# The recurrence's projections as four products of 32 weight columns

## The reference

```python
q  = einsum('mbtd,dk->mbtk', tx, w_q) * scale            # 128 columns, 4 heads of 32
k  = einsum('mbtd,mdk->mbtk', tx, w_k)
v  = einsum('mbtd,mdk->mbtk', tx, w_v)                   # 256 columns, 4 heads of 64
gk = log_sigmoid(einsum('mbtr,mrk->mbtk', einsum('mbtd,mdr->mbtr', tx, w_gk1), w_gk2) + b_gk) / 16
def step(S, inp):                                        # for each memory, batch and head
    qt, kt, vt, gt = inp
    S = S * exp(gt)[..., None] + kt[..., None] * vt[..., None, :]
    return S, einsum('...k,...kv->...v', qt, S)
```

## Time and profile before

| | us |
|---|---|
| median of three timed runs | 2658.96 |
| lowest and highest | 2658.64, 2659.07 |
| the profiled execution | 2684.99 |
| its span | 2683.3 |

### The profile page before, as it was taken

One profiled execution on the slowest core, in us unless ns is written; L12 is line 12 of the kernel. 1 busy time (PEld: TensorE's weight loads), 2 busy tenths in 40 slices (PEclk: granted clock), 3 DMA queues, 4 the chain that ended last, 5 costly groups with the idle time before them and its releaser, 6 DMA issues. The chain is left out here.

```text
span 2683.3 us, 111106 instructions
## 1 busy us (share of the span) xinstructions
PE 2124.7 (79%) x45872; PEld 1600.7 (60%) x45872; DVE 1836.9 (68%) x4507; ACT 1561.9 (58%) x3824; POOL 1531.6 (57%) x3168
## 2 busy tenths in 40 slices
PE   8788888888888888888868944389999998687793
PEld 5456566566566665556637734366766776565682
DVE  6578888887878887884544555276777777575456
ACT  5577777777777777772433322266666665454231
POOL 3357666666766666768554546544444444256452
PEclk9889999999999999999988965699999999789897
DMA  6911111111121111113346654301111111542546
GB/s 216 265 33 40 40 40 40 40 40 40 41 63 39 40 40 40 40 29 120 138 113 209 197 172 153 109 22 47 51 50 51 49 41 35 199 169 89 154 146 225
DMA packets 188851, 245.89 MB, mean 92 GB/s; under 512 B 41672, under 2 KB 144981, under 8 KB 187456
## 3 DMA queue, kind: packets, MB, share of 16 engines
q1 hardware_dynamic: 161824, 182.08, 22.7%
q0 software_dynamic: 19872, 50.41, 5.5%
q10 hardware_dynamic: 6656, 6.31, 0.8%
HBM read 136.08 MB, written 106.50 MB: 90 GB/s over the span
## 5 line engine op out<-in xcount | busy, mean ns | idle before, releaser
L666 ACT ACTIVATE at_E<-at_S,at_mn 128x1024 f32<-128x1024 f32 (+7 forms) x704 | 594.2, 847 | 211.3 <-DVE at_mn L737 178.2
L737 DVE TENSOR_REDUCE at_mn<-at_S 128x1 f32<-128x1024 f32 (+3 forms) x448 | 494.0, 1104 | 152.6 <-PE at_S L846 152.3
L846 PE MATMUL at_S<-am_sk,am_sq 96*32 96x512 bf16 (+3 forms) x4608 | 395.8, 350 | 1.1 <-ACT at_Tt L656 1.0
L887 PE MATMUL at_pcs<-at_E,at_c 128*32 128x256 f32 (+1 forms) x4864 | 375.7, 338 | 0.0
L605 POOL TENSOR_TENSOR at_kvo<-am_kh,am_vh 128x256 f32<-128x256 f32 x512 | 304.2, 628 | 0.0
L887 PEld LDWEIGHTS at_pcs<-at_E,at_c 128*32 128x32 f32 x4864 | 229.7, 109 | 41.2 <-issue 0.2
L1360 POOL DMA_INDIRECT expert_out<-m_ysb,m_dst x158 | 155.5, 984 | 139.3 <-issue 76.7
L887 PE MATMUL at_pcs<-at_Tt,at_c 128*32 128x128 f32 x1024 | 189.8, 274 | 42.3 <-ACT at_pcs_s L679 42.3
L590 POOL TENSOR_TENSOR at_half<-at_half 128x128 f32<-128x128 f32 (+4 forms) x640 | 185.6, 290 | 50.1
L864 PE MATMUL at_M<-am_ident,at_Tt 128*32 128x64 f32 x8192 | 154.5, 225 | 68.9 <-ACT at_kvr L691 43.1
L656 ACT ACTIVATE at_Tt<-at_S,at_mn 128x192 f32<-128x192 f32 x512 | 174.1, 428 | 48.3 <-DVE at_mn L725 48.1
(11 more groups left out here) (393 smaller groups left out, 5579.9 us busy)
## 6 DMA issues: line engine op xcount, KB each, us to landing
m_xg<-expert_rows SPq DMA_DIRECT2D x158, 129.0 KB
am_sq<-q_parts SPq DMA_DIRECT2D x192, 64.0 KB, 2.3
am_sk<-k_parts SPq DMA_DIRECT2D x192, 64.0 KB, 2.3
memory_rows<-m_blank SPq DMA_DIRECT2D x16, 516.0 KB
gl_hx<-memory_rows SPq DMA_DIRECT2D x32, 258.0 KB, 3.6
m_wgu<-in_f_wgu SPq DMA_DIRECT2D x2, 4096.0 KB
rt_yin<-expert_out SPq DMA_DIRECT2D x7, 1024.0 KB, 11.4
fn_yin<-expert_out SPq DMA_DIRECT2D x7, 1024.0 KB, 8.9
```

What stands on the lines that cost most here:

```text
L666: ins = nc.scalar.activation(E[:, at:at + w], S[v % NS_B][:, i * CW:i * CW + w], ACT.Exp, bias=mn[:, q, s, 1 + j:2 + j], scale=-1.0, accum ...
L737: nc.vector.tensor_reduce(mn[:, q, :, :].rearrange("p s k -> p (s k)")[:, at[0]:at[0] + 1], S[v % NS_B][:, 0:w], AX.X, ALU.min).then_inc(s ...
L846: ins = nc.tensor.matmul(S[v % NS_B][x, at:at + cw], sq[:, u, t * P + x.start:t * P + x.stop], sk[:, u, c0 + c:c0 + c + cw], start=True, s ...
L887: ins = nc.tensor.matmul(pcs[j * R:(j + 1) * R, cols[0]:cols[1]].rearrange("p (b c) -> p b c", c=P), lhsT, rhs, start=(n, j) not in touche ...
```

## The change

In the helper `two` each matmul is issued as four, one for every 32 columns of the stationary operand; each writes its own 32 partitions of the same PSUM tile. `STRIP` is 32. The moving operand is the same for all four. The calls of `two`, their order and the semaphores stay as they are; the increment rides on the last strip.

```diff
--- before.py
+++ after.py
@@ -2537,7 +2537,9 @@
 
             def two(out, lhs, rhs):
                 for k in range(KC):
-                    ins = nc.tensor.matmul(out, lhs(k), rhs(k), start=(k == 0), stop=(k == KC - 1))
+                    for t in range(0, P, STRIP):
+                        ins = nc.tensor.matmul(out[t:t + STRIP, :], lhs(k)[:, t:t + STRIP], rhs(k), start=(k == 0),
+                                               stop=(k == KC - 1))
                 return ins
 
             def rows_T(a):
```

## The result

The changed kernel takes 2685.6 us (median of 9 runs, 2672.59 to 2688.94) where the kernel before takes 2659.07 in the same comparison: ratio 1.0093, 95% interval 1.0077 to 1.011, 26.5 us slower. The forecast was 2659.5 with a range to 2672.

What follows compares the result with a forecast made beforehand. The prediction took the VectorE and ScalarE chain to set the pace, TensorE adding only when delayed. Query -2, first chunk's products -0.5, instruction supply +3 gave +0.5 us on 2658.96: 2659.5, range 2649 to 2672.

Steps and rivals of the forecast that it cites:

- the loads would stand alone: Last rival: in the edited products, strips run one after another, each weight load alone; 272 us more, 2930; chance 0.01.
- The clock stayed: Rival on TensorE in the recurrence: tighter groups keep the clock up, three waits of 3 us go; 2650; chance 0.10.
- VectorE's wait for the logarithm: Sign in the profile after: VectorE's idle for ScalarE's logarithm in the recurrence stays near 95 us.
- The gain of TensorE: Edited products in strips free 1.1 us per own chunk, 1.0 per shared one, 25.6 us over the loop, mostly hidden.
- the first rival: TensorE is the bound of the recurrence after all, so all 25.6 us count: 2633; chance 0.10.
- against this stands the supply of instructions: Cost term in the recurrence: 26 more instruction packets make TensorE pause; taken as +3 us, bounds 0 and 22.6.
- 26 x 0.87 = 22.6 us: Upper bound of the instruction supply cost in the recurrence: each of 26 new packets brings one unhidden pause of 0.87 us.
- 4.0 us for a packet: Mean spacing of instruction packets in the recurrence after the change, in place of 4.9; held well over the pauses seen.
- cover for 0.7 of a chunk: TensorE lacks cover in only some 7 of 23 us of a chunk, so 0.3 of the pauses count: 6.8 us.
- The third rival: Instructions come too late between the gate's end and the first half's scores: 11 to 14 us longer, 2672; chance 0.21.
- The test I set: VectorE's wait for scores in the recurrence stays near 30 us; below 15 means a gain, over 45 a loss.
- carried it over unchanged: The profiled execution's 26 us above the median of timed runs was kept: 2685.5 for the profile, 2659.5 for the median.

Runs made afterwards that it cites:

- x9: The kernel before, unedited, timed and profiled again on one of the faster chips: ratio 1.0001, profile 2660.31 us.
- x10: The changed kernel, unedited, timed and profiled again on one of the faster chips: ratio 1.0098 to the kernel before, profile 2685.55 us.
- x8: The changed kernel with the output products (lines 2670 and 2675) whole instead of in four strips, both halves of a chunk: ratio 1.0041 to the kernel before.
- x6: The kernel before with the output products (lines 2670 and 2675) whole instead of in four strips, both halves of a chunk: ratio 1.0066.
- x2: The kernel before with only the gate product in strips, on a chip where the kernel before takes 2677 or 2682 us (S): ratio 1.0024.
- x4: The kernel before with only the key product in strips, on a chip where the kernel before takes 2677 or 2682 us (S): ratio 1.0077.
- x7: The kernel before with 256 fulfilled waits, 128 instructions, added once ahead of the phase's first product: ratio 1.006.
- x5: The kernel before with 24 fulfilled waits behind each of the helper's 544 calls, 6528 more instructions: 3137.23 us, ratio 1.1807.
- x12: The kernel before with strips only in the first chunk's value product, 96 more instructions once, in front of the loop: ratio 1.0025.

## Why the prediction was wrong

**Right.** 49136 matmuls; 26 packets more in the whole program, 135 for 138 in the same 550 us; the strips overlap. By the rule of the Trainium skill, page "TensorE: Matmul & The Clock Gate", section "Part 3: Packing small matmuls — row/col tiling", as the prediction applied it, the loads would stand alone; the gate's 64 matmuls and 64 loads of 0.11 us took 1.86 us, so the rows do not agree with it. The clock stayed, 0.98 over the phase as in the earlier trace rows. VectorE's wait for the logarithm stayed (87.9 and 86.7 us in x9 and x10). The gain of TensorE was sized a little high: by the groups after, gate 0.13, query 0.07, key 0.4, value 0.13, 0.73 us for an own chunk where I had 1.1. Hardly any of it was to count, and x8 bears that out: its loop is no shorter than x6's. (TensorE was busy for 89.7% of the phase by the earlier trace rows, 493.34 of 550 us, and not for over 90% as the first rival says.)

**The step that failed** is "against this stands the supply of instructions", +3 us with an upper bound of 22.6. Measured, the gaps at packet ends went from 23.4 to 62.0 us, 38.6 more, TensorE's idle in them from 18 to 44 us, 26 more, and the loop got 23.2 us longer. "The trace has no row that ties one pause to one packet" was wrong too: the starts of the queue's packets were there. Three faults lie in the step:

- I let only the 26 new packets pause. A denser stream makes the old ones late as well: the share of ends that pause went from 23 of 112 to 69 of 135. So 26 x 0.87 = 22.6 us was no upper bound; the new idle alone is 26 us.
- I set 4.0 us for a packet against the length of a pause and found it ample. It has to be set against the time that a packet takes to be brought. Where a packet was run off in under 3.0 us, 21 of 27 ends paused in x9 and 41 of 43 in x10, and run plus pause then came to 3.6 us in the mean, eight of ten between 3.2 and 4.1; the closest two packets of the queue start 3.3 us apart in both. That is the supply, 3.3 to 4 us for a packet. Where it took over 4 us, 1 of 65 and 6 of 50 paused; from 3 to 4 us, 1 of 19 and 22 of 41. The whole products were the loose stretches: 4 to 16 matmuls in 2 us. Stretches over 5 us were 48 of 111 before and 9 of 134 after. The mean, 4.9 to 4.0 us, was close to that already, and the mean was all I looked at.
- I gave TensorE cover for 0.7 of a chunk. The loop's 23.2 us are 0.6 of the 38.6 us of new gaps and 0.9 of the 26 us of new idle, where I had let 0.3 through; they came in part through the key product and line 2687 to VectorE's state update (3.9 to 9.4 us), which I had counted as covered.

The third rival had the mechanism and the side, "decides once a packet's instructions are run faster than a packet can be brought", and was priced at 11 to 14 us by the same mistake, half of the new packets.

**The test I set** was misleading. VectorE's wait for scores, 30.1 in the earlier trace rows, was to go over 45 for a loss. It is 35.1 in the first profile after, which has none of the further gaps, while the profile before has 24 of them, as on an S chip. On one chip it is 15.0 to 33.9. I noted that the profiled execution was 26 us over the median, and "carried it over unchanged" in place of asking which rows the 26 us were in.

**Open.** Why the gate alone (x2) costs 6 us without more pauses, and the key alone (x4) 21 us, is not shown, and both stand on S chips, where the further gaps lie as well. What the 24 gaps on the S chips are, beyond their place beside GpSimd's stores, was not tried. How much each packet end costs by its place in the chunk was not measured; one shift of all of them was worth 7 us. None of the variants is faster than the kernel before by more than its interval.

## What to carry to other kernels

Where TensorE runs many small instructions, look at the time of each stretch of one instruction packet, not at the mean: here 62 of 70 packets of 256 instructions that it ran off in under 3 us were followed by a pause, and the long products between bursts of short ones seem to be what let the supply catch up. Cutting such a product into strips saves 0.1 to 0.2 us and takes the slack away; before doing so, count how many instructions the change adds per us of its surroundings. And when a profile stands 1% over the timed median, take both profiles on one chip before reading a difference of 1% from them.

## What the runs showed of the hardware that was not expected

- TensorE's pauses for instructions stand at every 256th of its instructions. A packet is 16 KB (6.03 MB in 368). No two of them started less than 3.2 us apart in the loop, in any profile, and a pause ended 2.1 to 3.3 us after a packet's start (all 69 in x10).
- A fulfilled semaphore wait as an instruction of its own took 0.106 us of TensorE's stream where they stood behind each other (x7, 128 in 13.7 us, and x5); in x5 each added 0.073 us to the kernel's time.
- The same kernel took 2658 to 2662 us on three chips and 2677 and 2682 on two; the profiles from the slower ones have gaps of 0.6 us in TensorE's scores beside GpSimd's indirect stores, 24 in the loop of the kernel before, where the others have none.
- A shift of 96 instructions, at no work of its own, was worth 7 us (0.25%) in x12.
